# Gathers of the first twelve batches issued in the attention answers, and three edits of the feed-forward, in one fused graph, attention and expert kernel

## What is computed

```python
xn = layernorm(x)
def graph(h):                               # for each edge type t, then summed
    for i in range(3):
        m = h @ conv_w[t, i]
        agg = segment_sum(m[src] * (edge_type == t), dst)
        h = gru(agg, h, wih[t], whh[t], bih[t], bhh[t])
x = x + leaky(layernorm(xn + sum_t graph_t(xn)))
      + attention_by_moments(xn)            # 8 heads, second-order expansion of softmax
xf = layernorm(x)
i2, w2 = top_k(xf @ Wg + bg, 2)             # 8 experts, softmax over the two chosen
out = x + sum_k w2[k] * (gelu(xf @ W1[i2] + b1) @ W2[i2] + b2)
```

## Time and profile before

| | us |
|---|---|
| median of three runs (3057.07 to 3064.43) | 3063.77 |
| profiled execution | 3079.78 |
| its span | 3078.1 |
| TensorE busy | 2647.3 (86%) |
| VectorE busy | 1593.7 (52%) |
| ScalarE busy | 642.6 (21%) |
| GpSimd busy | 1334.5 (43%) |

### The profile page before, as it was taken

How to read it: one execution, slowest core, us unless ns; L and a number is a source line. 1 busy time by engine, 2 the same in 40 slices (tenths; PEclk the granted TensorE clock), 3 DMA queues, 4 the chain that set the end, 5 groups by cost and what they waited for, 6 DMA issues and landing times. The chain is left out here.

```text
span 3078.1 us, 39296 instructions
## 1 busy us (share of the span) xinstructions
PE 2647.3 (86%) x13041; PEld 1704.6 (55%) x13041; DVE 1593.7 (52%) x3119; ACT 642.6 (21%) x1180; POOL 1334.5 (43%) x1375
## 2 busy tenths in 40 slices
PE   5898899669988989688999897798898875899997
PEld 3434455355555556454555555654445455788886
DVE  6798877335555555254555552466667684111110
ACT  3211100111111114111111114122212231333222
POOL 0000000356666661666666643666666600333433
PEclk8898999879999999799999998899999995999998
DMA  4300765434444442444444434433444413133223
GB/s 128 130 1 1 263 238 192 152 91 131 142 143 130 143 125 86 142 127 128 128 142 144 130 105 139 131 114 113 128 129 122 122 50 113 32 89 90 65 63 71
DMA packets 201473, 362.85 MB, mean 118 GB/s; under 512 B 27937, under 2 KB 156109, under 8 KB 201104
## 3 DMA queue, kind: packets, MB, share of 16 engines
q0 software_dynamic: 67776, 169.95, 20.1%
q1 hardware_dynamic: 129564, 186.48, 18.1%
q10 hardware_dynamic: 3956, 4.19, 0.5%
HBM read 293.37 MB, written 70.34 MB: 118 GB/s over the span
## 5 line engine op out<-in xcount | busy, mean ns | idle before, releaser
L1443 POOL DMA_INDIRECT g_ring<-h_rows,idx x780 | 768.2, 985 | 400.9 <-issue 199.3
L1114 PE MATMUL g_pagg<-g_onehot,g_ring 128*128 128x144 f16 x4704 | 425.7, 231 | 196.5 <-issue 187.8
L1114 PEld LDWEIGHTS g_pagg<-g_onehot,g_ring 128*128 128x128 f16 x4704 | 343.3, 100 | 452.7 <-issue 433.6
L1285 DVE TENSOR_TENSOR g_agg<-g_agg,g_pagg 128x288 f32 x585 | 265.4, 454 | 402.0 <-remote 233.1
L1443 POOL DMA_INDIRECT g_ring<-xn_rows,idx x390 | 386.6, 991 | 197.7 <-issue 102.3
L1288 DVE SCALAR_TENSOR_TENSOR g_onehot<-iota_keys,shift,keys 128x288 f16<-128x288 f16 x585 | 299.6, 513 | 0.6 <-issue 0.6
L1191 PE MATMUL g_pr<-g_agg,g_wc 128*128 128x448 f32 (+1 forms) x576 | 231.5, 524 | 15.2 <-issue 9.5
L1377 DVE SCALAR_TENSOR_TENSOR g_t<-g_ph,g_bh,g_rT 128x448 f32<-128x448 f32 (+1 forms) x144 | 89.9, 624 | 290.4 <-remote 209.2
L1191 PE MATMUL g_pz<-g_agg,g_wc 128*128 128x448 f32 (+1 forms) x576 | 230.8, 523 | 1.8 <-issue 1.7
L1191 PE MATMUL g_pr<-g_hT,g_wh 128*128 128x448 f32 (+1 forms) x576 | 226.0, 513 | 6.4 <-issue 6.3
L1191 PE MATMUL g_pz<-g_hT,g_wh 128*128 128x448 f32 (+1 forms) x576 | 221.6, 505 | 9.3 <-issue 6.3
(11 more groups left out here) (353 smaller groups left out, 3409.2 us busy)
## 6 DMA issues: line engine op xcount, KB each, us to landing
ma_R<-q_cols SPq DMA_DIRECT2D x27, 896.0 KB, 9.8
f_w<-in_L_ffn_W SPq DMA_DIRECT2D x16, 1024.0 KB, 7.7
h_cols<-g_hn SPq DMA_DIRECT2D x36, 448.0 KB
h_rows<-g_rows SPq DMA_DIRECT2D x36, 448.0 KB
g_hT<-h_cols SPq DMA_DIRECT2D x36, 448.0 KB
mix_R<-q_cols SPq DMA_DIRECT2D x15, 896.0 KB, 10.0
g_ring<-h_rows,idx POOLq DMA_INDIRECT x780
ma_R<-q_cols SPq DMA_DIRECT2D x9, 1120.0 KB, 5.6
```

Of the source, the lines that this page charges most:

```text
L1114: mm = e.matmul(pg[:, k * TYPES:(k + 1) * TYPES, :].rearrange("p t d -> p (t d)"), ring[:, slab, c, o:o + P], hot[:, c, :], start=(c == 0 ...
L1285: e.tensor_tensor(agg[:, :, bass.ds(o, DT)], agg[:, :, bass.ds(o, DT)], pagg[b % BANKS][:, :, :], ALU.add).then_inc(S["added"], 1)
L1443: e.indirect_dma_start(ring[:, b % SLABS, c, :], None, tables[s], bass.IndirectOffsetOnAxis(ap=idx[:, o:o + 1], axis=0)).then_inc(landed[b ...
```

## The change

1. **Gathers.** The ring of 12 batches no longer has memory of its own: it lies in that of `xnT`, which is kept until the graph steps end. The preliminary batch has a tile of its own. GpSimd issues the 24 gathers of batches 0 to 11 of the first step in the block of the attention answers and waits there until they have landed; in the first step its loop begins with batch 12.
2. **Gate weights.** ScalarE issues the loads of the gate's weights and bias at the block's start, in place of SP. TensorE waits for them before the transposes of tile 1, not before those of tile 0.
3. **Placement.** `dve_lanes` goes in eight chunks of 7 tiles, and TensorE's groups with it.
4. **Output copy.** SP copies rows 0 to 1561 and ScalarE rows 1562 to 3124, both when all is added.

```diff
+    with nc.sbuf_tensor("xnT", [P, KC, NP], F32) as xnT:
+        ring = xnT[:, :, :].rearrange("p k n -> p (k n)").bitcast(F16)[:, 0:SLABS * BATCH * 2 * C].rearrange("p (r b c) -> p r b c", r=SLABS, b=BATCH)
...
+            @block.gpsimd
+            def _(e):
+                for b in range(SLABS):
+                    for c in range(BATCH):
+                        o = FIRST + (b + 1) * BATCH + c
+                        e.indirect_dma_start(ring[:, b, c, :], None, rows_from, bass.IndirectOffsetOnAxis(ap=idx0[:, o:o + 1], axis=0)).then_inc(landed[b], 16)
+                for b in range(SLABS):
+                    e.wait_ge(landed[b], 16 * BATCH)
...
-        ring = sb("ring", [P, SLABS + 1, BATCH, 2 * C], F16)
+        pre_ring = sb("pre_ring", [P, BATCH, 2 * C], F16)
...
-                    for b in range(MB):
+                    for b in range(0 if s else SLABS, MB):
...
-            for j in range(4):
-                k, i = j // 2, j % 2 * HALF
+            for j in range(2 * PARTS):
+                k, i = j // PARTS, j % PARTS * PART
...
-                    e.dma_start(wg[:, :, :], A["L0_ffn_Wg"].rearrange("(k p) n -> p k n", p=P)).then_inc(S["gate_in"], 16)
-                    e.dma_start(bg[:, :], A["L0_ffn_bg"].rearrange("(a n) -> a n", a=1).to_broadcast([PT, XPT])).then_inc(S["gate_in"], 16)
...
-                e.dma_start(out[:, :], acc_rows[0:N, :]).then_inc(S["stored"], 16)
+                e.dma_start(out[0:HALF_OUT, :], acc_rows[0:HALF_OUT, :]).then_inc(S["stored"], 16)
...
-                e.wait_ge(S["gate_in"], 32)
                 for i in range(TILES):
+                    if i == 1:
+                        e.wait_ge(S["gate_in"], 32)
...
             @block.scalar
             def _(e):
+                e.dma_start(wg[:, :, :], A["L0_ffn_Wg"].rearrange("(k p) n -> p k n", p=P)).then_inc(S["gate_in"], 16)
+                e.dma_start(bg[:, :], A["L0_ffn_bg"].rearrange("(a n) -> a n", a=1).to_broadcast([PT, XPT])).then_inc(S["gate_in"], 16)
...
+                total = e.value_load(first_tile[0:1, XPT:XPT + 1], min_val=1, max_val=NFT)
+                e.wait_ge(S["added"], total * 2 + 2)
+                e.dma_start(out[HALF_OUT:N, :], acc_rows[HALF_OUT:N, :]).then_inc(S["stored_high"], 16)
+                e.wait_ge(S["stored_high"], 16)
```

More of the change, by code:

```diff
@@ L138, in gps_layer_kernel, with mix @@
     edges = {"keys": keys, "bases": bases, "main_at": main_at, "shift": shift, "idx0": idx0, "idx1": idx1, "tab": tab}
[L139 to L142, removed]
+    landed = [nc.alloc_semaphore(f"g_landed{r}") for r in range(SLABS)]
+    with nc.sbuf_tensor("xnT", [P, KC, NP], F32) as xnT:
+        ring = xnT[:, :, :].rearrange("p k n -> p (k n)").bitcast(F16)[:, 0:SLABS * BATCH * 2 * C].rearrange("p (r b c) -> p r b c", r=SLABS, b=BATCH)
+        with nc.sbuf_tensor("acc_mix", [PT, TILES, C], F32) as acc:
+            mix(nc, A, acc, xnT, ident, ones, acc_rows, edges, table0, hT0, ring, landed)
+        gnn(nc, A, tables, [hT0] + hTs, idx0, idx1, keys, bases, main_at, shift, tab, iota_keys, ident, acc_rows, xf, ring, landed)
     ffn(nc, A, acc_rows, ident, ones, xf, out)
-def mix(nc, A, acc, xnT, ident, ones, acc_rows, edges, rows_to, cols_to):
+def mix(nc, A, acc, xnT, ident, ones, acc_rows, edges, rows_to, cols_to, ring, landed):
     q_cols = nc.dram_tensor("q_cols", [KC, P + P // 2, NP], F32).ap()
@@ L1107, in pre_rounds, with count_batch @@
             return rounds, number
-        def count_batch(e, pg, slab, hot, start_sem):
+        def count_batch(e, pg, rows, hot, start_sem):
             for c in range(BATCH):
@@ L1113, in count_batch @@
                         o = part * C + k * P
[L1114 removed]
+                        mm = e.matmul(pg[:, k * TYPES:(k + 1) * TYPES, :].rearrange("p t d -> p (t d)"), rows[:, c, o:o + P], hot[:, c, :],
                                       start=(c == 0 and part == 0 and k == 0), stop=(c == BATCH - 1 and part == 1 and k == KC - 1), skip_group_check=True)
@@ L1847, in _ @@
                 e.matmul(pk, ones[0:1, 0:PT], offset[:, :, :].rearrange("p t x -> p (t x)"), start=False, stop=True).then_inc(S["ranks"], 1)
-                for j in range(4):
+                for j in range(2 * PARTS):
                     e.wait_ge(S["lane"], 4 * j + 4)
-                    for i in range(HALF):
-                        mm = e.matmul(found, lane[j % 2][:, i, :], row_and_weight[j % 2][:, i, :], start=(j == 0 and i == 0), stop=(j == 3 and i == HALF - 1))
+                    for i in range(PART):
+                        mm = e.matmul(found, lane[j % 2][:, i, :], row_and_weight[j % 2][:, i, :], start=(j == 0 and i == 0), stop=(j == 2 * PARTS - 1 and i == PART - 1))
                     mm.then_inc(S["found"], 1)
```

41 lines of the change are left out of this document (20 added, 21 removed).

## The result

The changed kernel takes 3036.19 us (median, 3033.54 to 3042.43) against 3063.67 for the kernel before: ratio 0.9911, interval 0.9895 to 0.9927, which is 27.5 us less. The forecast was 3050 with a range of 3038 to 3065. The profiled execution took 3035.37 us (span 3033.7). That is 44.4 less than the profiled one of before, but that one had been 16 above its own median, so the two profiles are compared stage by stage, and their total is not.

What follows compares the result with a forecast made beforehand. TensorE was taken to bound the answers and the graph steps. Lead -20.1, answers +7.9, gate weights -0.9, placement -0.7 and output copy -0.2 gave -14.0, from 3063.77 to 3049.8 us; forecast 3050, range 3038 to 3065.

Steps and rivals of the forecast that it cites:

- What bounds: Attention answers and graph steps: TensorE is the bound, so what it gets done sooner moves the end.
- Lead of step 0, -20.1: Start of the first graph step: with 24 gathers moved out, the aggregate's first matmul comes at 620.0 instead of 640.1.
- Answers, +7.9: Attention answers: the early gathers hold TensorE back from 333.0 to 347.1, costing 7.9 us; loads inside that.
- rival B: Attention answers: gathers do not hold TensorE back, only the loads' 1.5 us remain; 3043.4, chance 0.25.
- Behind the lead, nothing: Rest of step 0: nothing on GpSimd is late next, so the lead's gain is carried to the end unchanged.
- Parts 2 to 4, -1.8: Feed-forward: gate weights -0.9, placement in eight chunks -0.7, output copy in two -0.2.
- the bias on ScalarE's queue: Feed-forward's start: gate bias issued at 2542.3, there at 2546.6, 0.4 sooner; with tile 0's transposes done by then, -0.9.
- the placement: Feed-forward, lanes in eight chunks: VectorE ends 1.0 later, TensorE's last group 1.7 shorter, net -0.7.
- the two copies: Output at the end: bound by transfer, so two halves at once take as long as the whole, -0.2.
- The sum: Whole kernel: -20.1 + 7.9 - 0.9 - 0.7 - 0.2 = -14.0, from 3063.77 to 3049.8.
- Rival D: Output copy: halves spread over too few DMA engines; with 3 engines +19.5, in all 3069.3, slower; chance 0.08.
- rival C: Step 0's lead and answers: hole not cured or the answers pay it back; -4.9, taken as 3060; chance 0.23.

Runs made afterwards that it cites:

- half_width: Kernel before, but the second of the two matmuls of each gate and half in a unit multiplies only half of the columns: 3045.41 us, ratio 0.9951.
- paced_before: Kernel before, with GpSimd pausing three times in the lead of all three steps, no gathers moved: 3054.70 us, ratio 0.9981.
- paced_after: Whole change, with GpSimd also pausing three times in the lead of steps 1 and 2: 3039.11 us, ratio 0.9924 to the kernel before.
- credit8: Whole change, but GpSimd asks for free slabs eight at a time, sixteen gathers in a run: 3491.28 us, ratio 1.1301 to the kernel before.

## Why the prediction was wrong, point by point

**What bounds.** "What TensorE gets done sooner in either stage therefore moves the end" fails in the graph steps (in the answers no run tested it). This is the step that failed. A busy share of 89% looked like a bound; half_width took 166 us of TensorE's busy time away for a gain of 15. What changes a step's length is GpSimd's gathers, with the pauses between them: closing the leads' holes was worth 6.4 us (paced_before) and nothing (paced_after), and leaving out gathers was worth 1.10 to 1.15 us each. In step 0 of the profiled pair GpSimd took 586.8 us from its first gather to its last before and 557.4 after, 29.4 less, close to the 30.2 of 24 gathers, while its pauses add up to the same, 94.4 and 94.8. At the 1.15 us of the gathers left out, 24 are worth 27.6, and the whole change gained 27.5, 25.0, 23.4 and 20.7 us in four sessions. The prediction priced the gap in the lead and put the gathers' own time in the step at nothing.

**Lead of step 0, -20.1.** It measured -24.9 (61.8 to 36.9). The add of batch 3 was forecast for 607.8 and came at 606.87; from it to the last add it took 8.8 us instead of the 11.7 taken from the hole itself, part of which was hold. That a long run of gathers goes with TensorE held back was confirmed by the pauses in paced_before and by credit8, for the steps and not for the answers. That the gain was kept to the end was right for another reason than mine: not because the lead was shorter, but because 24 gathers were out of the step. On the chip without the hold the lead did not change and the step gained 16.4 all the same. That the lead's 24.9 is nearly the whole gain is luck.

**Answers, +7.9.** This is the largest mis-sized term of the sum, but not all of the miss: the range's low end had B's 1.5 in its place, with a lead at -25, and the time still fell below it. "If it starts 20 us in, it covers 333.0 to 347.1": it did not start. The answers grew by 2.4 us in the profiled pair, and by 1.6 in the means over all profiles. TensorE's matmuls there are fewer for the time, 62 in the first 30.3 us against 52 in 17.4 in step 1, which fits rival B's condition (long matmuls), though no run varied it. The gathers took 48.4 us instead of 30.3, which cost nothing. B's answer term of 1.5 was right; I gave the case 0.25.

**Behind the lead, nothing.** Step 0 was 4.6 us shorter in its rest. The 30.2 us of issue that went, less the 12 for which GpSimd waits for batch 0, leave 18, and the pauses of 4.07 in the former lead and of 6.71 just behind it went too.

**Parts 2 to 4, -1.8.** They measured 0: ratio 1.0002 alone, and 1.0 us longer in the profiled pair within a spread of 2.9. Of the steps, the bias on ScalarE's queue landed later than forecast (7.3 us after its issue instead of 4.4), the placement gained 0.1 where 0.7 was forecast, and the two copies took 13.5 us from their issue to the end against 12.8.

**The sum.** -24.9 + 2.4 - 4.6 + 1.0 = -26.1, against -27.5 measured. Rival B with its 3043 would have been 7 off, and nearest. Rival D fell: both halves of the output went in equal packets. Of rival C one half was seen, but in the steps and not in the answers: where a lead is relieved and the gathers stay, it is paid back.

**What stays open.** Why one session shows no hold and all the others do, with the same program. What a gather and TensorE's signals share: the number of TensorE's instructions is not it alone, instructions of ScalarE count a little, and clearing tiles on GpSimd costs about half of what gathers cost. Each execution here was recorded by the profiler. That the recording of instructions is itself what they share is a rival that no run rules out, and whether the hold exists without recording wasn't tried.

## What to carry to other kernels

A busy share near 90% is no proof of a bound: look at the engine that feeds it, add up its issue and its pauses over a whole step, and see whether the sum is the step's length. An isolated hole is worth only what the loop behind it doesn't give back; before pricing it, ask which engine's total becomes less. Here the gathers that left the loop had to be priced, not the gap that one sees. And run the kernel before on more than one chip, and more than once, before explaining an odd stall: 270 us lay between two sessions here.

## What the runs showed of the hardware

The same program took 2794 us in one session and 3060 to 3086 in the others, on other chips, nearly all of it in the graph steps, where GpSimd issues gathers one behind the other: steps of 552 to 566 us against 649 to 658, the answers and the feed-forward alike within 3 us. In the slower sessions TensorE issues single matmuls at multiples of 0.7 us in the later part of a run of gathers in the steps, and its signals reach the other engines when GpSimd pauses; in the answers a run of 24 gathers left TensorE busy for all of its 39.1 us. Every gather of the answers that took 1.6 to 4.8 us of GpSimd instead of 0.96 overlapped a TENSOR_TENSOR of VectorE. The loads of the queries took 11.5 us from issue to landing beside the gathers instead of 9.8 (median), and TensorE did 62 matmuls in the first 30.3 us instead of 65. Where the hold is seen, asking for eight slabs at once, so that gathers came in runs of sixteen instead of some eight, made the kernel 13% slower.
